# The small constant of three layer norms moves from an addition into the variance aggregate

## The reference

```
x = layernorm(x + self_attention(x))              # 16 heads of 64, causal
x = layernorm(x + cross_attention(x, ctx, mask))  # 16 heads of 8
x = layernorm(x + mixture_of_experts(x))          # 8 experts of width 256, two of them per token
layernorm(x) = (x - mean(x)) / sqrt(var(x) + 1e-05)   # over the 128 features
```

## Time and profile before

| | |
|---|---|
| median of three runs | 233.37 us |
| the profiled execution, its own time | 233.06 us |
| span of the trace in that execution | 231.0 us |
| around the span (233.06 − 231.0) | 2.06 us |
| PE, PE weight loads, DVE, ACT, POOL busy | 98%, 89%, 83%, 71%, 44% |
| granted TensorE clock | 1.0 of 2.4 GHz |
| DVE instructions | 954 |

### The profile page before, as it was taken

One profiled execution on the slowest core, in us unless ns is written; L12 is line 12 of the kernel. 1 busy time (PEld: TensorE's weight loads), 2 busy tenths in 40 slices (PEclk: granted clock), 3 DMA queues, 4 the chain that ended last, 5 costly groups with the idle time before them and its releaser, 6 DMA issues.

```text
span 231.0 us, 6982 instructions
## 1 busy us (share of the span) xinstructions
PE 225.9 (98%) x2274; PEld 205.9 (89%) x2274; DVE 192.1 (83%) x954; ACT 164.9 (71%) x552; POOL 102.0 (44%) x162
## 2 busy tenths in 40 slices
PE   8999999999999999999999999999999999999992
PEld 8999888997978988978978988789999999999992
DVE  3897798997889889989899879989898565766984
ACT  3768988898999979999989999697476333333001
POOL 4387738796396568922978351231200000100112
PEclk9999999999999999999999999999999999999999
DMA  6998000000000000000002200000000000000000
GB/s 189 362 363 314 10 0 0 4 3 1 3 1 3 0 6 3 0 3 1 1 4 64 121 3 3 3 0 4 0 3 0 1 3 0 4 23 0 26 23 24
DMA packets 7011, 9.10 MB, mean 39 GB/s; under 512 B 1088, under 2 KB 5824, under 8 KB 6592
## 3 DMA queue, kind: packets, MB, share of 16 engines
q1 hardware_dynamic: 4320, 7.09, 8.7%
q10 hardware_dynamic: 2656, 1.57, 2.3%
HBM read 8.14 MB, written 0.52 MB: 37 GB/s over the span
## 4 chain that ended last, share of the span: by engine, by line
PE 96%; DVE 1%; issue 1%; POOL 1%; ACT 0%; POOLq 0%; ACTq 0%; DVEq 0%
PE bank L1545 13%; PE bank L1443 11%; PE bank L1445 10%; PE bank L1444 10%; PE bank L2043 9%; PE bank L1527 7%; PE bank L1554 7%; PE bank L1595 6%; PE bank L1563 4%; PE bank L1538 3%; PE bank L1611 2%; PE bank L1482 2%; PE bank L1483 2%; PE bank L1484 2%; PE bank L1570 2%; PE bank L2053 1%
## 5 line engine op out<-in xcount | busy, mean ns | idle before, releaser
L525 ACT ACTIVATE probs_s<-masked_s,nmax_s 128x128 f32<-128x128 f32 x128 | 49.8, 396 | 3.6 <-DVE nmax_s L839 2.1
L311 POOL TENSOR_TENSOR probs_s<-probs_s,rec_sum_s 128x512 f32<-128x512 f32 x32 | 33.1, 1040 | 35.0 <-DVE rec_sum_s L846 34.8
L586 ACT ACTIVATE silu<-bank 128x256 f32<-128x256 f32 x54 | 20.1, 384 | 30.3 <-PE bank L1445 28.4
L528 ACT ACTIVATE probs_c<-masked_c,nmax_c 128x128 f32<-128x128 f32 x128 | 40.3, 396 | 1.6 <-DVE nmax_c L839 1.4
L1443 PE MATMUL bank<-ctx_hi,gu_hi 128*128 128x256 f32 x128 | 38.7, 302 | 0.0
L1444 PE MATMUL bank<-ctx_lo,gu_hi 128*128 128x256 f32 x128 | 35.7, 279 | 0.0
L1445 PE MATMUL bank<-ctx_hi,gu_lo 128*128 128x256 f32 x128 | 35.7, 279 | 0.0
L839 DVE CUSTOM_DVE_ANT_0 masked_c<-bank,mask_add 128x128 f32<-128x128 f32 x128 | 29.0, 286 | 4.6 <-PE bank L1538 3.9
L839 DVE CUSTOM_DVE_ANT_0 masked_s<-bank,causal 128x128 f32<-128x128 f32 x128 | 29.2, 285 | 1.2 <-PE bank L1527 1.0
L503 POOL TENSOR_TENSOR mv<-mv,minus_half 128x1 f32<-128x1 f32 x7 | 3.8, 556 | 55.2 <-DVE mv L1388 55.2
L1443 PEld LDWEIGHTS bank<-ctx_hi,gu_hi 128*128 128x128 f32 x128 | 24.3, 190 | 0.7 <-DVE qk_a L969 0.3
(11 more groups left out here) (180 smaller groups left out, 591.4 us busy)
## 6 DMA issues: line engine op xcount, KB each, us to landing
raw<-in_gateT SPq DMA_DIRECT2D x1, 1024.0 KB, 8.2
raw<-in_upT SPq DMA_DIRECT2D x1, 1024.0 KB, 12.1
down_sb<-in_down SPq DMA_DIRECT2D x1, 1024.0 KB, 5.2
raw<-in_wvT SPq DMA_DIRECT2D x1, 512.0 KB, 5.6
ctxT_all<-in_ctxT SPq DMA_DIRECT2D x1, 512.0 KB, 6.9
masked_c<-in_mask ACTq DMA_DIRECT2D x1, 512.0 KB, 11.9
wo_sb<-in_woT SPq DMA_DIRECT2D x1, 512.0 KB, 6.1
x_tok<-in_x ACTq DMA_DIRECT2D x1, 512.0 KB, 11.2
```

What stands on the lines that cost most here:

```text
L311: pool.tensor_tensor(probs_s[:, g % 2], probs_s[:, g % 2], spread(rec_sum_s[:, 4 * g:4 * g + 4], 2, S), ALU.mult).then_inc(normed[g], 1)
L525: last = act.activation(probs_s[:, g % 2, i, :], masked_s[:, g % 2, i, :], ACT.Exp, scale=-1.0, bias=nmax_s[:, h:h + 1], accum_out=rsum_s[ ...
L528: last = act.activation(probs_c[:, g % 2, i, :], masked_c[:, g % 2, i, :], ACT.Exp, scale=-1.0, bias=nmax_c[:, h:h + 1])
L586: act.activation(silu[:, i % NS, :], g, ACT.Silu).then_inc(silued, 1)
```

## The change

`bn_stats` still writes two triples. They now lie in the first six of nine numbers, and the last three hold a triple that never changes: count 0, mean 0, and count times variance 128 × 1e-05. `bn_aggr` reads all nine. The counts sum to 128 as before, and the third triple adds 128 × 1e-05 / 128 = 1e-05 to the variance. The additions L855 and L1388 go, with their semaphores, and POOL reads the variance where `bn_aggr` put it. The statistics tiles of the three layer norms become one tile `stats` of 4 × 9 numbers per partition in place of 6 + 6 + 12, and two memsets at the head of DVE's list fill the constant triples.

```diff
-        stat1 = sb("stat1", [P, 6])
+        stats = sb("stats", [P, 2 + TB, 9])
+        stat1, stat2, stat3 = stats[:, 0, :], stats[:, 1, :], stats[:, 2:2 + TB, :]
...
-            def root(var_done, pow_done, mv, n):
-                pool.wait_ge(var_done, n + 1)
-                pool.tensor_tensor(mv[:, 3:4], mv[:, 2:3], minus_half[:, 0:1], ALU.pow).then_inc(pow_done, 1)
+            def root(aggr_done, pow_done, mv, n):
+                pool.wait_ge(aggr_done, n + 1)
+                pool.tensor_tensor(mv[:, 3:4], mv[:, 1:2], minus_half[:, 0:1], ALU.pow).then_inc(pow_done, 1)
...
+            dve.memset(stats[:, :, 6:8], 0.0)
+            dve.memset(stats[:, :, 8:9], D * EPS)
             dve.memset(cvp[:], 0.0).then_inc(pad_set, 1)
...
-                dve.bn_stats(stat, res).then_inc(stat_done, 1)
+                dve.bn_stats(stat[:, 0:6], res).then_inc(stat_done, 1)
                 dve.wait_ge(stat_done, n + 1)
                 dve.bn_aggr(mv[:, 0:2], stat).then_inc(aggr_done, 1)
-                dve.wait_ge(aggr_done, n + 1)
-                dve.tensor_scalar(mv[:, 2:3], mv[:, 1:2], EPS, None, ALU.add).then_inc(var_done, 1)
...
-                dve.bn_stats(stat3[:, tb, :], acc[:, c % 2, tb, :]).then_inc(stat3_done, 1)
+                dve.bn_stats(stat3[:, tb, 0:6], acc[:, c % 2, tb, :]).then_inc(stat3_done, 1)
...
-            variance_of_y(LAST - 1, 0)
-            variance_of_y(LAST - 1, 1)
...
-            variance_of_y(LAST, 1)
```

More of the change, by code:

```diff
@@ L153, in build_decoder @@
         res2 = sb("res2", [P, D])
-        stat2 = sb("stat2", [P, 6])
         mv2 = sb("mv2", [P, 4])
@@ L228, in build_decoder @@
         cat_done = [sem(f"cat_done{a}") for a in range(2)]
-        (wo_s, res1_done, stat1_done, aggr1_done, var1_done, pow1_done, x1_ready, x1bo_done,
+        (wo_s, res1_done, stat1_done, aggr1_done, pow1_done, x1_ready, x1bo_done,
          x1T_ps, x1T_evac, cq_proj, cq_evac, cq_lower) = [sem(n) for n in (
-             "wo_s res1_done stat1_done aggr1_done var1_done pow1_done x1_ready x1bo_done "
+             "wo_s res1_done stat1_done aggr1_done pow1_done x1_ready x1bo_done "
              "x1T_ps x1T_evac cq_proj cq_evac cq_lower").split()]
-        (oc_evac, oct_ps, rec_c, ccat_done, ccatT_ps, ccatT_evac, wo_c, res2_done, stat2_done, aggr2_done, var2_done, pow2_done,
+        (oc_evac, oct_ps, rec_c, ccat_done, ccatT_ps, ccatT_evac, wo_c, res2_done, stat2_done, aggr2_done, pow2_done,
          x2_ready, x2T_ps, x2T_evac, logit_ps, logit_evac, x2_split) = [sem(n) for n in (
-             "oc_evac oct_ps rec_c ccat_done ccatT_ps ccatT_evac wo_c res2_done stat2_done aggr2_done var2_done pow2_done "
+             "oc_evac oct_ps rec_c ccat_done ccatT_ps ccatT_evac wo_c res2_done stat2_done aggr2_done pow2_done "
              "x2_ready x2T_ps x2T_evac logit_ps logit_evac x2_split").split()]
         (r_step, r_exp_in, r_exp, dense_ready, gated, silued, gate_done, hid_done, down_ps, combined,
-         stat3_done, aggr3_done, var3_done, pow3_done, y_ready) = [sem(n) for n in (
+         stat3_done, aggr3_done, pow3_done, y_ready) = [sem(n) for n in (
              "r_step r_exp_in r_exp dense_ready gated silued gate_done hid_done down_ps combined "
-             "stat3_done aggr3_done var3_done pow3_done y_ready").split()]
+             "stat3_done aggr3_done pow3_done y_ready").split()]
         def qk_of(a, pair, which, i):
@@ L408, in _ @@
             normalise(3, 1)
-            root(var1_done, pow1_done, mv1, 0)
+            root(aggr1_done, pow1_done, mv1, 0)
             normalise(2, 1)
@@ L415, in _ @@
             add_out_bias(0)
-            root(var1_done, pow1_done, mv1, 1)
+            root(aggr1_done, pow1_done, mv1, 1)
             split_gu(1)
@@ L426, in _ @@
             normalise(0, 3)
-            root(var1_done, pow1_done, mv1, 2)
+            root(aggr1_done, pow1_done, mv1, 2)
             add_out_bias(2)
@@ L436, in _ @@
             normalise(0, 4)
-            root(var2_done, pow2_done, mv2, 0)
+            root(aggr2_done, pow2_done, mv2, 0)
             normalise(1, 4)
-            root(var1_done, pow1_done, mv1, 3)
+            root(aggr1_done, pow1_done, mv1, 3)
             padded_v(3)
@@ L449, in _ @@
             normalise(1, 5)
-            root(var1_done, pow1_done, mv1, 4)
-            root(var2_done, pow2_done, mv2, 1)
+            root(aggr1_done, pow1_done, mv1, 4)
+            root(aggr2_done, pow2_done, mv2, 1)
             add_out_bias(4)
@@ L456, in _ @@
             normalise(0, 6)
-            root(var2_done, pow2_done, mv2, 2)
+            root(aggr2_done, pow2_done, mv2, 2)
             split_x2(0)
             normalise(1, 6)
-            root(var1_done, pow1_done, mv1, 5)
+            root(aggr1_done, pow1_done, mv1, 5)
             own_k(5)
@@ L466, in _ @@
             padded_v(5)
-            root(var2_done, pow2_done, mv2, 3)
+            root(aggr2_done, pow2_done, mv2, 3)
             own_k(7)
@@ L471, in _ @@
             normalise(1, 7)
-            root(var1_done, pow1_done, mv1, 6)
+            root(aggr1_done, pow1_done, mv1, 6)
             normalise(2, 7)
@@ L477, in _ @@
             add_out_bias(6)
-            root(var2_done, pow2_done, mv2, 4)
-            root(var1_done, pow1_done, mv1, 7)
+            root(aggr2_done, pow2_done, mv2, 4)
+            root(aggr1_done, pow1_done, mv1, 7)
             split_x2(3)
@@ L482, in _ @@
             add_out_bias(7)
-            root(var2_done, pow2_done, mv2, 5)
+            root(aggr2_done, pow2_done, mv2, 5)
             split_x2(4)
             split_x2(5)
-            root(var2_done, pow2_done, mv2, 6)
+            root(aggr2_done, pow2_done, mv2, 6)
             split_x2(6)
-            root(var2_done, pow2_done, mv2, 7)
+            root(aggr2_done, pow2_done, mv2, 7)
             split_x2(7)
@@ L1405, in _ @@
                     if c and e == 1:
-                        for part in (sums_of_y, mean_of_y, variance_of_y):
+                        for part in (sums_of_y, mean_of_y):
                             for tb in range(TB):
```

15 lines of the change are left out of this document (5 added, 10 removed).

## The result

The changed kernel takes 232.34 us, the median of six runs (232.1 to 232.61), beside 233.32 for the kernel before on the same chip (232.96 to 233.5). The ratio is 0.9955, with a 95% interval of 0.9945 to 0.9965. A second measurement of the same kernel on another chip gave 232.61 beside 233.33, 0.9969 [0.9957, 0.9981].

What follows compares the result with a forecast made beforehand. PE was taken to bound the kernel up to its last product, then the last layer norm's chain. From the profiled 233.06: −0.18 end, −0.08 body, 0 start, 232.80; plus 0.31 to the median, 233.1 us; range 232.6 to 233.6.

Steps and rivals of the forecast that it cites:

- The end: After PE's last matmul: addition leaves the path, 0.19 us, less 0.01 for the longer `bn_aggr`; gain 0.18, bounds 0.10 to 0.19.
- the port rule: DVE two-port and GpSimd operations exclude each other for whole instructions; some 0.04 us better at the last power, left out.
- The start: Two added memsets at the head of DVE's list, at most 0.18 us, hidden by DVE's 2.27 us idle; counted zero.
- The body: 22 more additions go, over 4 us of DVE's time beside PE's work; PE gets back 0.08 us.
- the 320 ns lost at the transposes: PE's total loss at the transposes of x1 and x2, 8 × 25 + 8 × 15; a quarter taken as gain.
- rival (a): PE gets back the body's full bound, 0.5 us, as DVE's list pulls everything forward; 232.7 us, chance 0.22.
- the prediction's own sign: PE's last matmul ends within 0.3 us of 226.87; if more than 0.3 earlier, rival (a) is right.
- (b): At the end, `bn_aggr` with a third triple runs longer and eats the addition's 0.19 us; 233.4 us, chance 0.09.
- (c): Slower: earlier chains put normalisations under POOL's long operations, 0.24 us each; three give 233.9 us; chance 0.07.
- Range: Whole kernel: 232.6 us, just under rival (a), to 233.6, over (b) and into the first collision of (c).

Runs made afterwards that it cites:

- e: The kernel before with two one-number memsets, which nobody reads, added at the head of DVE's list; ratio 1.0009 [0.9993, 1.0024] against the kernel before.
- a: The kernel before with its tiles placed as in the changed kernel, every instruction as before; ratio 0.9975 [0.9963, 0.9987] against the kernel before.
- b: The changed kernel with every tile at its address of before; ratio 0.9971 [0.9958, 0.9984] against the kernel before.
- j: b with the additions put back behind `bn_aggr`, their result read by nobody; ratio 0.9995 [0.9984, 1.0007] against the kernel before.
- h: No layer, only a loop of gate and up matmuls, moving operand shifted in 32-byte steps; starts 114.0 ns apart at 128 bytes, 117.8 at 0.

## Why the prediction was off

**The end: right, a little small.** Forecast −0.18, measured −0.20 in the length from the last matmul on. The addition and its wait went as worked out. `bn_aggr` over nine numbers takes 196 ns in the mean where it took 182, so 14 and not 10 for the triple. The groups of the profile after (busy, mean ns):

```profile
L856 DVE BATCH_NORM_AGGREGATE mv<-stats 128x2 f32<-128x9 f32 x16 | 3.1, 196 | 0.5
L1593 PE MATMUL bank<-ident,x 128*128 128x128 f32 x8 | 2.3, 283 | 0.0
L1576 PE MATMUL bank<-ident,ctxT_all 128*128 128x128 f32 x8 | 2.3, 288 | 0.0
```

What I left out came: the power takes 0.567 us instead of 0.603, and 0.04 is what the port rule had given. The rule itself still fails by its own measure: L1428 runs to 227.14 + 0.32 = 227.46, and a power of 0.547 that got nothing before then would end at 228.01; it ends at 227.87. So the 0.04 came, and the runs do not show why.

**The start: right.** The two memsets take 0.07 and 0.06 and are done at 0.89, and the lower halves of the weights start at 4.35, against 4.37 in the earlier trace rows:

```profile
0.79 0.07 DVE L800 MEMSET stats<- 128x8 f32 x1 [0.79 <-PEq L2104]
0.83 0.06 DVE L801 MEMSET stats<- 128x4 f32 x1
...
4.35 0.88 DVE L809 SCALAR_TENSOR_TENSOR w_lo<-raw,w_hi 128x256 fp32r<-128x256 f32 x1 [2.19 <-ACT w_hi L516]
```

Counted as time they cost nothing. Counted as places in the list they moved every later instruction by two. In e that alone was worth 0.11 us in the body and cost 0.17 at the end, and it did not occur to me.

**The body: this step failed.** The term was 0.08 us, a quarter of the 320 ns lost at the transposes, and the body moved by 0.73. In its place the runs show these terms:

- 0.38 us from the place of a tile (a: 0.377). The sum had no term for it. The diff shows three `sb` lines fewer and one more, and I read them as bookkeeping.
- About 0.17 from the position of one pair in DVE's list (b and e between 98 and 111 us). The sum had no term for it either.
- 0.07 from the additions as links of the chain (j against e). I had said that mostly the order of DVE's list and not the chain decides when x1 and x2 are normalised, and priced what the transposes get back by it at 0.08.
- At most 0.08 from the additions as time in the list (b against j, less the place at record 319), not shown apart from the spread of profiles. I had found DVE 88% busy from 130 to 167 us and given this to rival (a), at 0.22, with a bound of 0.5.

The two last are 0.15 together at most, twice the term; 0.03 of the 0.73 has no name. The transposes of x1 and x2 gave back 8 × 17 + 8 × 2 = 152 ns, by the rows above and the earlier trace rows, not 80; a quarter was too small a share, and PE got more back elsewhere. By the prediction's own sign rival (a) would be right, as PE's last matmul ends at 226.25 instead of 226.87, more than 0.3 earlier. But its 232.7 is 0.36 above the 232.34 measured, and its reason was mostly wrong: PE got back 0.73, more than the bound of 0.5, and of that DVE's shorter list gave at most 0.15. The forecast of a gain was right in its direction partly by luck, since most of the gain had no term.

**The rivals (b) and (c): wrong.** `bn_aggr` did not grow by a programme of its own. Normalising x1 takes 338 ns at the shortest, 344 in the middle and 607 at the longest, against 336, 346 and 586 in the earlier trace rows, so the two engines met about as before.

**Range.** The range was built from terms for the instructions that change. It had no term for the addresses and for the position of the code, though both are changed by nearly every edit, and here they were about 0.55 of the 0.93 us.

## What to carry over

Two kernels that differ in a tile's size or in two instructions differ in addresses and in code position too, and in a kernel bound by matmuls that alone can be worth as much as the edit: compare with a kernel that has only the new layout, and with one that has only the new count. Where PE is busy throughout, read the distance between the starts of equal matmuls, not their length; if it changes between two builds, try the moving tile's address before looking for a wait. Before a small step is called the cost of an instruction, follow it along the time axis: here half of what looked like the additions' time in the list arose at one place, long before most of them ran.

## What the hardware showed beyond that

- In a bare loop the 128 x 256 matmuls start every 114.0 ns at one of eight 32-byte steps of the moving operand modulo 256 bytes, and every 116.7 to 119.8 ns at the others (h). In the layer the short pace is 113.3 to 113.8 ns.
- The profiles of one kernel differ by 0.5 us and more ahead of the body, and a good part of it can lie between 4 and 7 us. In the profile of the kernel before, the projections start every 0.12 us from 5.77 on; in that of a they start every 0.21 us until 6.9 and only then every 0.12, nearly twice as long at first, and the body begins 0.62 later (15.791 against 15.173). The view prints a granted clock of 1.00 in both from 4 to 8 us, but the first record of the clock in the trace, 1.00 and so 2.4 GHz, begins only at 5.67 us in the kernel before and at 7.14 us in a; ahead of it there is no record, and 1.00 is what the view prints for that. The slow starts end with it in both. That fits the lower level, 1.2 GHz, ahead of it, though no record says so. PE's timeline of a:

```profile
6.69 0.41 PE L1442 MATMUL bank<-x_hi,w_hi 128*128 128x256 f32 x1
6.90 0.40 PE L1443 MATMUL bank<-x_lo,w_hi 128*128 128x256 f32 x1
7.12 0.30 PE L1444 MATMUL bank<-x_hi,w_lo 128*128 128x256 f32 x1
7.26 0.28 PE L1442 MATMUL bank<-x_hi,w_hi 128*128 128x256 f32 x1
7.38 0.28 PE L1443 MATMUL bank<-x_lo,w_hi 128*128 128x256 f32 x1
```

- Left open: why the pace depends on the address, whether it is the distance to the weights or the moving address alone that counts, and why the same kernel keeps or loses the short pace behind a wait.
